# Cross-attention and mixture of experts on one core: k's low part, q's conversion, two transfers and the feed-forward's first bias take other places

## The reference

```python
def attention(x, y):                      # x is layernormed; per batch 256 rows
    q = ln(x @ Wq + bq)                   # 16 heads of 32, normalised per head
    k, v = ln(y_main @ Wk + bk), y_main @ Wv + bv      # 240 keys
    kd, vd = ln(y_dca @ Wkd + ..), y_dca @ Wvd + ..    # 16 more keys
    ctx = softmax(q k^T * s) v + softmax(q kd^T * s) vd
    return ctx @ Wo + bo
def ffn(x):                               # x is layernormed
    top2 = top_k(softmax(mean(x, rows) @ gate_W.T), 2)  # 2 of 6 experts per batch
    h = gelu(x @ W1[e] + b1[e])           # 512 -> 352
    return sum_e w_e * (h @ W2[e] + b2[e])
x = x + attention(layernorm(x), ctx)
x = x + ffn(layernorm(x))
```

## Time and profile before

| | us |
|---|---|
| median of 3 runs | 1132.83 (1128.11 to 1137.46) |
| profiled execution, whole | 1133.56 |
| its span, first to last instruction | 1131.7 |
| TensorE busy | 968.7 (86%) |
| VectorE busy | 797.6 (70%) |
| ScalarE busy | 638.8 (56%) |
| GpSimd busy | 294.9 (26%) |
| mean granted TensorE clock | 0.93 |

### The profile page before, as it was taken

How to read it: one execution, slowest core, us unless ns; L and a number is a source line. 1 busy time by engine, 2 the same in 40 slices (tenths; PEclk the granted TensorE clock), 3 DMA queues, 4 the chain that set the end, 5 groups by cost and what they waited for, 6 DMA issues and landing times. The chain is left out here.

```text
span 1131.7 us, 17393 instructions
## 1 busy us (share of the span) xinstructions
PE 968.7 (86%) x5020; PEld 649.3 (57%) x5020; DVE 797.6 (70%) x1706; ACT 638.8 (56%) x1658; POOL 294.9 (26%) x203
## 2 busy tenths in 40 slices
PE   0756899999999999999999998664599999999998
PEld 0323545545555545555555555332588888888887
DVE  2736778787787787788788777334877777768774
ACT  0223887787888788778778778665322313122131
POOL 0474315315415415424414513000000000000000
PEclk9978899899999899999999999767699999999999
DMA  7015624634634634733634543676011111111110
GB/s 260 28 31 129 147 72 125 152 85 124 151 89 119 157 85 117 178 79 110 171 81 112 151 95 84 145 253 224 2 55 56 56 56 38 55 56 56 56 37 38
DMA packets 56413, 116.41 MB, mean 103 GB/s; under 512 B 13944, under 2 KB 22392, under 8 KB 56120
## 3 DMA queue, kind: packets, MB, share of 16 engines
q1 hardware_dynamic: 53760, 115.16, 37.0%
q10 hardware_dynamic: 2616, 0.79, 0.3%
HBM read 47.24 MB, written 17.30 MB: 57 GB/s over the span
## 5 line engine op out<-in xcount | busy, mean ns | idle before, releaser
L471 POOL TENSOR_TENSOR vs<-vs,neg_half 128x16 f32<-128x16 f32 x66 | 196.1, 2980 | 367.3 <-DVE vs L920 367.3
L798 ACT ACTIVATE sc<-sc,nm 128x240 f32<-128x240 f32 x512 | 222.9, 441 | 66.0 <-DVE ed L968 65.5
L963 DVE TENSOR_REDUCE pm<-sc 128x64 f32<-128x1024 f32 x128 | 156.2, 1221 | 38.2 <-PE sc L625 34.7
L578 PE MATMUL ring<-wq,xT 128*128 128x512 f32 x256 | 144.6, 718 | 21.2 <-ACT xT L766 16.1
L1388 ACT ACTIVATE hb<-hb 128x352 f32<-128x352 f32 x64 | 31.8, 497 | 227.8 <-DVE hb L1444 227.8
L625 PE MATMUL sc<-KS,QS 96*128 96x256 f32 x512 | 107.7, 335 | 44.3 <-ACT sc L798 39.4
L807 ACT ACTIVATE pt<-sc 128x1024 f32<-128x1024 f32 x128 | 124.0, 1024 | 29.4 <-PE sc L646 29.4
L625 PEld LDWEIGHTS sc<-KS,QS 96*128 96x128 f32 x512 | 75.2, 200 | 92.8 <-ACT sc L798 61.3
L591 PE MATMUL ring<-wkv,cT 128*128 128x512 f32 (+1 forms) x256 | 124.4, 611 | 0.9 <-ACT kdT L779 0.9
L678 PE MATMUL ring<-wo,ot 128*128 128x512 f32 x256 | 122.8, 604 | 0.7 <-DVE ot L1010 0.7
L798 ACT ACTIVATION_READ_ACCUMULATOR sc<-sc,nm 128x1 f32 x512 | 109.2, 213 | 0.0
(11 more groups left out here) (137 smaller groups left out, 1632.6 us busy)
## 6 DMA issues: line engine op xcount, KB each, us to landing
KS<-k_hi SPq DMA_DIRECT2D x128, 128.0 KB, 2.3
QS<-q_hi SPq DMA_DIRECT2D x128, 128.0 KB, 3.0
xin<-in_x_dram SPq DMA_DIRECT2D x16, 512.0 KB, 4.0
KS<-k_lo SPq DMA_DIRECT2D x64, 128.0 KB, 2.3
QS<-q_lo SPq DMA_DIRECT2D x64, 128.0 KB, 2.9
xres<-in_x_dram SPq DMA_DIRECT2D x16, 512.0 KB, 3.3
x_scratch<-xres SPq DMA_DIRECT2D x16, 512.0 KB, 4.7
x<-x_scratch SPq DMA_DIRECT2D x16, 512.0 KB, 3.2
```

What stands on the lines that cost most here:

```text
L471: pool.tensor_tensor(w, w, neg_half[0:rows, :], ALU.pow).then_inc(rstd, 1)
L578: last = pe.matmul(bank[:, :], xT[:, kc, t * P:(t + 1) * P], wq[:, kc, :], start=(kc == 0), stop=(kc == KC - 1))
L798: last = act.activation(s, s, ACT.Exp, bias=nm[:, t, h:h + 1], accum_out=den[:, t, h:h + 1])
L963: dve.tensor_reduce(pieces, s.rearrange("p h (c n) -> p h c n", n=DCA), AX_X, ALU.max, negate=True).then_inc(g_max, 1)
```

## The change

Four places move; no operation is added or taken away.

- VectorE, attention: `k_hi` stays behind the sixth maximum, `k_lo` moves behind the eighth, and so does the first sum of the extra keys (`dca_sums(b, 0)`).
- ScalarE, attention: the conversion of q (QT0, QT1) moves from ahead of the last two probabilities to behind them.
- SyncE, attention: the load of x moves ahead of the copies of q, the store of x2 behind the first four of them.
- Feed-forward: VectorE loads the experts' numbers and adds the first bias ahead of the next batch's statistics, and takes the second bias ahead of its normalisation. TensorE does the first expert's full chunks of the first output tile (six matmuls) ahead of the second tile's hidden transposes. The banks follow from the new list.

```diff
--- before.py
+++ after.py
@@ -422,17 +422,19 @@
                 sp.wait_ge(sh_hi, b + 1)
                 for a in range(2):
                     shift_rows(sp, par, a, s_hi, 0)
+            if step in STATS:
+                load_x(b + 4)
             if step in KEYED:
                 sp.wait_ge(split, 4 * (b + 1) + 3)
                 stack_rows(QS, 1 - par, q_hi, 0, q_in)
+            if step in WOUT:
+                wait_evac(sp, step, "WO1", b)
+                sp.dma_start(x2_dram[b - 1], xres[:, :, :]).then_inc(x2_st, 16)
+            if step in KEYED:
                 stack_rows(QS, 1 - par, q_hi, 2, q_in)
                 sp.wait_ge(split, 4 * (b + 1) + 4)
                 stack_rows(QS, 1 - par, q_lo, 1, q_in)
-            if step in STATS:
-                load_x(b + 4)
             if step in WOUT:
-                wait_evac(sp, step, "WO1", b)
-                sp.dma_start(x2_dram[b - 1], xres[:, :, :]).then_inc(x2_st, 16)
                 sp.wait_ge(x2_st, 16 * b)
             if step in ATTN:
                 sp.dma_start(xres[:, :, :], x_t[b]).then_inc(r_ld, 16)
@@ -871,6 +873,9 @@
             if attn:
                 probabilities(step, b, 4)
                 probabilities(step, b, 5)
+            if attn:
+                probabilities(step, b, 6)
+                probabilities(step, b, 7)
             if proj:
                 wait(act, split, 4 * (b + 1) + 4)
                 affine_out(step, b, "QT0", qf[:, 0:2, :], affine_q)
@@ -881,9 +886,6 @@
                     square("p1", -2, f"DK{c}", 4 + c, dca_values(c))
                 for j in range(2):
                     affine_out("p1", -2, f"KD{j}", kdT[:, 2 * j:2 * j + 2, :], affine[:, 4:6])
-            if attn:
-                probabilities(step, b, 6)
-                probabilities(step, b, 7)
 
         walk(act, body)
 
@@ -986,24 +988,30 @@
             dve.tensor_tensor(by_head(kb[0:ROWS[c], c, :]), by_head(bank[0:ROWS[c], :]),
                               kv_half(bkv_b[0:ROWS[c], :], 0), ALU.add).then_inc(taken(step, f"K{c}"), 1)
 
-        def split_parts(m, n, whole, hi, lo, stacked):
+        def split_high(m, whole, hi, stacked):
 
             wait(dve, stacked, STACKED * m)
             dve.tensor_copy(hi[:, :, :], whole[:, :, :]).then_inc(split, 1)
+
+        def split_low(m, n, whole, hi, lo):
             dve.wait_ge(split, 4 * m + n + 1)
             dve.tensor_tensor(lo[:, :, :], whole[:, :, :], hi[:, :, :].bitcast(F32),
                               ALU.subtract).then_inc(split, 1)
 
         def split_q(m):
 
-            split_parts(m, 2, qf, q_hi, q_lo, q_in)
-
-        def split_k(step, b):
+            split_high(m, qf, q_hi, q_in)
+            split_low(m, 2, qf, q_hi, q_lo)
+
+        def split_k_high(step, b):
 
             for name in ("KT0", "KT1"):
                 wait_evac(dve, step, name, b)
             dve.wait_ge(kd_rdy, b + 2)
-            split_parts(b + 1, 0, kf, k_hi, k_lo, k_in)
+            split_high(b + 1, kf, k_hi, k_in)
+
+        def split_k_low(b):
+            split_low(b + 1, 0, kf, k_hi, k_lo)
 
         def ctx_out(step, b, g):
             bank = wait_full(dve, step, f"PV{g}", b)
@@ -1039,11 +1047,14 @@
                 group_max(b, 4)
                 group_max(b, 5)
             if keyed:
-                split_k(step, b)
-            if attn:
-                dca_sums(b, 0)
+                split_k_high(step, b)
+            if attn:
                 group_max(b, 6)
                 group_max(b, 7)
+                dca_sums(b, 0)
+            if keyed:
+                split_k_low(b)
+            if attn:
                 dca_sums(b, 1)
             if keyed:
                 split_q(b + 1)
@@ -1167,7 +1178,7 @@
 
 
 
-    BODY = ["H0", "H1", "H2", "HT0", "H3", "XT0", "XT1", "HT1", "HR", "OUT0", "GT", "OUT1"]
+    BODY = ["H0", "H1", "H2", "HT0", "H3", "XT0", "XT1", "OUT0", "HT1", "HR", "GT", "OUT1"]
     NEXT = ["XT0", "XT1", "GT"]
     u = Units(8, [("pro", NEXT, -1, 1), ("first", BODY, 0, 1), ("body", BODY, 1, B - 2),
                   ("last", [n for n in BODY if n not in NEXT], B - 1, 1)])
@@ -1300,12 +1311,12 @@
                                         hb[:, TOP * t + e, (FC - 1) * P:FF], ident[:, :])
             last.then_inc(full[u.bank(step, "HR")], 1)
 
-        FULL_CHUNKS = [(e, fc) for e in range(TOP) for fc in range(FC - 1)]
+        FULL_CHUNKS = [[(e, fc) for fc in range(FC - 1)] for e in range(TOP)]
         LAST_CHUNKS = [(e, FC - 1) for e in range(TOP)]
 
         def output(step, b, ex, t, chunks):
 
-            if chunks is FULL_CHUNKS:
+            if chunks is FULL_CHUNKS[0]:
                 bank = begin(pe, step, f"OUT{t}", b)
                 wait_evac(pe, step, f"HT{t}", b)
                 if t == 0 and step == "first":
@@ -1319,7 +1330,7 @@
                 for i, (hp, wp) in enumerate(PASSES):
                     last = pe.matmul(bank[:, :], hT[hp][0:rows, e, fc, t * P:(t + 1) * P],
                                      w2[wp][0:rows, bass.ds(ex[e], 1), fc, :].rearrange("p a n -> p (a n)"),
-                                     start=(chunks is FULL_CHUNKS and n == 0 and i == 0),
+                                     start=(chunks is FULL_CHUNKS[0] and n == 0 and i == 0),
                                      stop=(chunks is LAST_CHUNKS and n == TOP - 1 and i == 2),
                                      skip_group_check=True)
             if chunks is LAST_CHUNKS:
@@ -1343,13 +1354,15 @@
                 x_transposes(step, b, 0)
                 x_transposes(step, b, 1)
             if ffn:
+                output(step, b, ex, 0, FULL_CHUNKS[0])
                 h_transposes(step, b, 1)
                 last_chunks(step, b)
-                output(step, b, ex, 0, FULL_CHUNKS)
+                output(step, b, ex, 0, FULL_CHUNKS[1])
             if nxt:
                 gate_logits(step, b)
             if ffn:
-                output(step, b, ex, 1, FULL_CHUNKS)
+                output(step, b, ex, 1, FULL_CHUNKS[0])
+                output(step, b, ex, 1, FULL_CHUNKS[1])
                 wait_evac(pe, step, "HR", b)
                 for t in range(T):
                     output(step, b, ex, t, LAST_CHUNKS)
@@ -1459,6 +1472,9 @@
                         gv[par][:, e:e + 1], (x2[par] if e == 0 else xo)[:, t, :], ALU.mult, ALU.add)
                     last.then_inc(res, 1)
 
+            if ffn:
+                ex = [dve.value_load(idx[par][0:1, e:e + 1], min_val=0, max_val=NE - 1) for e in range(TOP)]
+                bias(0, ex)
             if does_next:
                 dve.wait_ge(x_ld[nxt], 16 * (half + par + 1) if step != "pro" else 16)
                 for t in range(T):
@@ -1472,11 +1488,9 @@
                 for n in range(NE):
                     low_parts(n)
             if ffn:
-                ex = [dve.value_load(idx[par][0:1, e:e + 1], min_val=0, max_val=NE - 1) for e in range(TOP)]
-                bias(0, ex)
+                bias(1, ex)
                 if does_next:
                     row_norm()
-                bias(1, ex)
                 bias(2, ex)
                 hidden_low(0)
                 if step == "first":
```

## The result

The changed kernel takes 1103.81 us, the median of 4 runs (1101.77 to 1107.63), against 1132.28 us before (4 runs beside it, 1128.11 to 1137.46). The ratio is 0.9755, with a 95% interval from 0.9728 to 0.9781: 28.5 us less, where 21.4 were forecast. The predicted 1111 us is 7 us too high; the time lies inside the range of 1103 to 1122, by 0.8 us at its low end.

The account below looks back on a forecast made before the run. TensorE was taken to bound both phases, so only its standstills count. Gains of 14.0 (feed-forward body steps), 2.7 (first and last batch), 3.5 (attention) and 1.2 (k) sum to 21.4 us, giving 1111 us, range 1103 to 1122.

Parts of the forecast that it names:

- First wait of feed-forward: Body step, TensorE's first hidden transposes waiting for a GELU behind late biases: 0.82 us lost, 0.8 booked as gain.
- Second wait: Body step, second hidden transposes 0.35 us late for the fourth GELU; six output matmuls moved there remove it.
- What comes in its place: Feed-forward body step: new costs of 0.18 us, 0.1 possible wait for the second tile's hidden values, 0.08 for another switch.
- First and last batch: Feed-forward's end batches: earlier bias 0.65 and filled wait about 1.0 in the first, 1.1 in the last; 2.7 us.
- End of the attention step: Last probabilities start before q's conversion, so first scores come earlier: 0.25 us a step, 3.5 us over 14 steps.
- k's low part: VectorE, ahead of the seventh maximum: moving it gains nothing in body steps, 1.2 us once in the batch before the last.
- SyncE's queue: Attention: last q copy lands 2.8 us later against 3.3 of slack, 0.5 us early; nothing booked.
- The clock: TensorE's granted clock, which the forecast can't price; 5 us allowed for it.
- (a): q lands 4.3 us later, 1.0 over the slack, in eleven attention steps; 11 us go: 1122. Chance 0.13.
- (c): SyncE's transfers queue by full landings, 8.8 us against 3.3 of slack; first scores 5.5 late a step: 1171. Chance 0.04.
- (b): Feed-forward keeps about half its waits, 0.5 us in each of 14 steps; 7 us go: 1118. Chance 0.14.
- (d): Attention step's end held by the first maximum and its exponentials, so only feed-forward pays: 1115. Chance 0.10.

Follow-up runs that it names:

- e4_ffn_dve: Kernel before the change with only VectorE's new feed-forward order (biases ahead of statistics and normalisation); 1114.74 us, ratio 0.985.
- e3_ffn_pe: Kernel before the change with only TensorE's new feed-forward order (first expert's outputs ahead of the second tile's hidden transposes); 1125.12 us, ratio 0.993.
- e6_no_q: Changed kernel with ScalarE's conversion of q put back ahead of the last two probabilities; 1109.81 us, ratio 0.978 to before.
- e11_k_only: Kernel before the change with both feed-forward edits and, of the attention edits, only the later k_lo and first extra-key sum; 1112.06 us, ratio 0.979.
- e2_attn: Kernel before the change with only the edits of the attention phase; 1126.51 us, ratio 0.994.
- e5_no_sp: Changed kernel with SyncE's old queue order (x load and x2 store behind all copies of q); 1104.89 us, ratio 0.975 to before.
- e8_first: Changed kernel, first feed-forward batch re-ordered: second weights' high parts on ScalarE before the first GELU, fourth bias before the low parts, TensorE's old order; 1102.06 us.
- e10_qlow: e8_first with VectorE taking q's low part behind the shift's two parts instead of ahead of its transposes; 1106.35 us, ratio 0.974 to before.
- e1_ffn: Kernel before the change with only the two feed-forward edits (VectorE's and TensorE's order); 1111.11 us, ratio 0.981.

## Why the prediction was right, and where it was off

The direction, the main mechanism (feed-forward's two waits) and the order of the terms held; the sum was 7 us short, most of it in feed-forward. The attention phase came near its forecast partly by luck. By the prediction's own steps:

- **First wait of feed-forward, 0.82 us.** Right: 0.85 and 0.06 for the restart. `e4_ffn_dve` measured 0.90.
- **Second wait, 0.35.** Too small. It was got by counting eight transposes at 0.12 us, 0.96 in all, and they need 0.79 before the next unit can start; the wait was 0.52, and 0.06 for the restart.
- **What comes in its place, 0.18.** Nearly right, 0.14: 0.08 for the matmuls in two pieces and 0.06 behind the gate, which may be the forecast wait for the second tile's low part (0.1, "a tie") but is not listed as one. That the 0.08 was also booked is luck, since it came from a misreading: the 921.20 of the earlier trace rows is where the chain of waits resumes, and the first output matmul starts at 920.96, 0.85 behind the transposes and not 1.09. `e3_ffn_pe` measured 0.43 for these two items together. The step: 1.34, not 1.0, 4.7 us in 14 steps, and the second wait is the larger part of that. This is the term that was mis-sized: 1.34 x 14 = 18.7 lies above even its upper bound of 16.4, which counted the two waits as 0.82 and 0.35.
- **First and last batch, 2.7.** 5.0. The last is right (1.2 for 1.1). In the first batch the shift of a body step, 0.65, was used, but the first bias moved by 3 us: before, it stood 2.98 behind the end of the low parts, after it follows at once.

```profile
803.21 1.27 DVE L1465 BATCH_NORM_STATS2 f_st<-x 128x6 f32<-128x512 f32 x2
...
806.19 0.53 DVE L1444 TENSOR_TENSOR hb<-f_ring,b_b 128x352 f32<-128x352 f32 x1 [1.38 <-issue]
```

```profile
795.22 1.81 DVE L1429 TENSOR_TENSOR w_lo<-w_lo,w_hi 128x1024 fp32r<-128x1024 f32 x2
796.96 0.51 DVE L1457 TENSOR_TENSOR hb<-f_ring,b_b 128x352 f32<-128x352 f32 x1
```

- **End of the attention step, 0.25.** 0.22 and 0.19 at TensorE's rows there, which `e6_no_q` takes back. In the length of a step the same places differ by 0.1 at most, so the 3.5 us are not shown, and the bound of 0 is not excluded.
- **k's low part, nothing in body steps.** Half wrong. In the batch before the last it gave 1.35 (1.2 forecast), which the last batch took back at a lower clock (79.46 us for the two before, 79.72 after). In body steps "nothing" holds only while the slow stretch keeps TensorE from coming early to lt. The prediction named as its cover the projections; the cover was their slow clock. At full clock it is worth 0.76, by one step of `e11_k_only`.
- **SyncE's queue, 0 with 0.5 us to spare.** Right to 0.1 in the step shown: 2.7 us later for 2.8, slack 0.6 for 0.5; the other steps have 0 to 0.7. Taking the edit back costs nothing, making q later costs its lateness. The 2.8 was a middle between 1.3 and 4.4, and the 0.5 of slack hung on it: that it held so closely is luck.
- **The clock, ±5.** This is where the attention phase gained most. Its first 13 steps are 10.3 us shorter, and 0.25 a step would be 3.3 of that. Three long steps before and one after are worth some 5 to 6 us with the slow steps behind them (an estimate from the 1.7, 0.7, 0.5 and 0.2 above), and two steps at 1.00 after were 40.08 and 40.39. Whether the edits bring this about is open. For it: `e2_attn`, `e5_no_sp`, `e8_first` and the changed kernel, which have both q's and k's edit, have seven to ten steps of 40.9 to 41.2 us in a row, and those without one of the two at most three; and `e2_attn` gave 8.0 us, more than the local terms. Against it: one profile each, of kernels whose long steps come and go. With the old attention order four profiles had 3, 0, 2 and 0 long steps and 619.2 to 623.5 us from first to last lt; with all attention edits three had 1 each and 613.4 to 615.6. The means differ by 7.2 us, where 0.25 a step and the 1.35 give 5.

None of the rivals happened as a whole. (a) and (c) needed the first scores to wait for q, and they don't. (b) is excluded by the rows and the 40.00 busy of 40. That only feed-forward pays, (d), is excluded by `e2_attn`, whose interval ends at 0.996; its reason, that the end of the step is held by something else, is not, since no step length shows the 0.25.

## What to carry to other kernels

A gap costs what lies from start to start, less the same pair without a wait; the listed idle time is its lower bound, here by 0.16 and 0.25 us. A "no gain, covered by other work" must say whether the cover is as long at each clock; the cover here was a projection at 1.2 GHz. A step's length must be compared at the same place of the clock's pattern: the shortest of nine steps in a row is below the shortest of three, whatever the edit. And before an instruction is moved behind another on VectorE, follow every reader of what then comes later: in `e10_qlow` the reader was a queue with at most 0.7 us of slack.

## What the runs showed of the hardware that was not expected

- The two loads of expert numbers leave VectorE 1.38 to 1.76 us of idle when they follow the statistics, and none behind 5.3 us of low parts or within a wait of 1.37 us for TensorE. Why they are hidden there and not behind the statistics is not shown.
- A faster order meets a slower clock: the steps after can take 40.08 to 40.39 us, but in 12 of the first 14 TensorE was at 1.2 GHz for a part, and nine of them took 40.93 to 41.10. With the attention order of before, steps at 1.00 and at 0.96 were equally long (41.23 in `e1_ffn`, 41.20 before).
- A 128 KB copy of q's low part lands after 4.0 us with x and the store between the copies, and after 2.9 us without; x and the store themselves landed no later (4.0 and 4.3 against 4.1 and 4.7).
